# Cross-attention, second pass: blocks 2 to 32 score all 8 key tiles in one go, then weigh their own 8, with nothing carried into the next block

## What is computed

```python
q = ln @ Wq
kv = concatenate([xn, ln]) @ Wkv
k, v = split(kv)                       # 8 heads of 64 each
sim = einsum('bhid,bhjd->bhij', q / scale, k)
sim = sim - max(sim, axis=-1)
attn = softmax(sim, axis=-1)
out = einsum('bhij,bhjd->bhid', attn, v)
out = rearranged(out) @ Wout
```

## Time and profile before

| | |
|---|---|
| median of 3 runs | 2656.38 us (2655.33 to 2661.38) |
| the profiled execution: its own time | 2653.46 us |
| its span, first to last instruction | 2651.8 us |
| mean granted TensorE clock | 0.969 of full |
| TensorE busy | 2490.5 us (94%) |
| VectorE busy | 1809.0 us (68%) |
| ScalarE busy | 1122.2 us (42%) |
| GpSimd busy | 592.2 us (22%) |

### The profile page before, as it was taken

How to read it: one execution, slowest core, us unless ns; L and a number is a source line. 1 busy time by engine, 2 the same in 40 slices (tenths; PEclk the granted TensorE clock), 3 DMA queues, 4 the chain that set the end, 5 groups by cost and what they waited for, 6 DMA issues and landing times.

```text
span 2651.8 us, 33253 instructions
## 1 busy us (share of the span) xinstructions
PE 2490.5 (94%) x11614; PEld 1681.0 (63%) x11618; DVE 1809.0 (68%) x1885; ACT 1122.2 (42%) x1366; POOL 592.2 (22%) x404
## 2 busy tenths in 40 slices
PE   6999989988776999999999999999898899999998
PEld 5778877654334777776655555555586777777775
DVE  5878855499988677778976666666445766666665
ACT  2334422466344222222255555555233455455543
POOL 4555544488842211111100000000000000000000
PEclk9999998999877999999999999999898899999999
DMA  7667755722021343343233232232112255666663
GB/s 276 231 237 259 264 153 171 258 72 72 2 101 42 127 169 148 127 182 136 96 124 108 96 96 73 96 108 84 64 64 115 104 219 214 237 229 230 216 218 137
DMA packets 124235, 394.70 MB, mean 149 GB/s; under 512 B 23728, under 2 KB 39292, under 8 KB 97136
## 3 DMA queue, kind: packets, MB, share of 16 engines
q1 hardware_dynamic: 95584, 326.82, 34.8%
q10 hardware_dynamic: 28560, 66.66, 7.2%
HBM read 304.14 MB, written 89.30 MB: 148 GB/s over the span
## 4 chain that ended last, share of the span: by engine, by line
PE 79%; DVE 8%; DMA 5%; POOL 3%; issue 3%; ACT 2%; ACTq 0%; SPq 0%; DVEq 0%; POOLq 0%
PE ps L2109 18%; PE ps L2110 17%; PE ps L2111 17%; PE ps L2496 10%; PE ps L2506 9%; PE ps L2403 3%; DMA w_halves<-unit_lo 3%; DVE ps L1642 2%; POOL work L951 1%; PE ps L2757 1%; DMA wT_lo<-w_halves 1%; DMA sh_raw<-in_s_parts 1%; DMA x_res<-in_x 1%; POOL work L932 1%; DVE ln_st L1512 1%
## 5 line engine op out<-in xcount | busy, mean ns | idle before, releaser
L1862 DVE TENSOR_TENSOR sums<-sums,pT 128x1024 f32<-128x1024 f32 x272 | 319.2, 1222 | 194.0 <-ACT pT L1341 192.9
L1800 DVE SCALAR_TENSOR_TENSOR peak<-ps,rs_all,peak 128x1024 f32<-128x1024 f32 x272 | 335.7, 1279 | 93.9 <-PE ps L2403 93.6
L1341 ACT ACTIVATE pT<-ps,rs_all 128x1024 f32<-128x1024 f32 x272 | 284.8, 1111 | 230.8 <-PE ps L2496 184.9
L2506 PE MATMUL ps<-pT,values 128*64 128x512 f32 x1088 | 256.4, 602 | 0.0
L2226 PE MATMUL ps<-work,ident 128*128 128x512 f32 x256 | 130.3, 641 | 33.6 <-POOL work L932 18.6
L1001 POOL TENSOR_TENSOR cT_lo<-cT_raw,cT_hi 128x512 fp32r<-128x512 f32 x60 | 77.6, 1293 | 352.1 <-ACT cT_hi L1290 352.1
L2506 PEld LDWEIGHTS ps<-pT,values 128*64 128x64 f32 x1088 | 68.8, 136 | 132.9 <-issue 112.0
L1996 DVE TENSOR_TENSOR rgu_lo<-rgu_raw,rgu_hi 128x2048 fp32r<-128x2048 f32 x64 | 143.9, 2289 | 5.1 <-ACT rgu_hi L1424 5.0
L894 POOL TENSOR_TENSOR ctx_lo<-ctx_raw,ctx_hi 128x512 fp32r<-128x512 f32 x64 | 105.2, 1643 | 131.7 <-DVE ctx_hi L1547 131.7
L1642 DVE TENSOR_TENSOR_SCAN ps<-ps,work 128x1024 f32<-128x1024 f32 x50 | 114.3, 2285 | 13.2 <-ACT ps L1213 11.2
L1028 POOL TENSOR_SCALAR ln_ve<-ln_mv 128x1 f32<-128x1 f32 x4 | 1.5, 379 | 537.0 <-DVE ln_mv L1513 537.0
(11 more groups left out here) (470 smaller groups left out, 6429.9 us busy)
## 6 DMA issues: line engine op xcount, KB each, us to landing
rgu_raw<-in_r_gate_up SPq DMA_DIRECT2D x64, 1024.0 KB, 4.8
rd_raw<-in_r_down SPq DMA_DIRECT2D x32, 1024.0 KB, 4.8
sh_raw<-in_s_parts SPq DMA_DIRECT2D x32, 768.0 KB, 4.3
key_rows<-key_hi SPq DMA_DIRECT2D x17, 1024.0 KB, 3.9
key_rows<-key_lo SPq DMA_DIRECT2D x17, 1024.0 KB, 6.0
value_rows<-values SPq DMA_DIRECT2D x17, 1024.0 KB, 8.9
ctxT_raw<-in_ctx_T SPq DMA_DIRECT2D x16, 1024.0 KB, 6.8
ctx_raw<-in_ctx SPq DMA_DIRECT2D x16, 1024.0 KB, 8.5
```

The lines of the kernel that those rows point to most:

```text
L1341: nc.scalar.activation(pT[:, i], ps[:, b:b + 2], ACT.Exp, scale=rs_all[:, bass.ds(c * KT + attend_tile(j, i)[1], 1)]).then_inc(s4_exp.sem, 1)
L1800: nc.vector.scalar_tensor_tensor(peak[:, p], ps[:, b:b + 2], rs_all[:, bass.ds(c * KT + kt, 1)], peak[:, p], ALU.mult, ALU.max).then_inc(s ...
L1862: nc.vector.tensor_tensor(sums[:, p], sums[:, p], pT[:, i], ALU.add).then_inc(s4_sum.sem, 1)
L2506: done = nc.tensor.matmul(ps[e * DK:(e + 1) * DK, 6 + p], values[:, s, kt, h * DK:(h + 1) * DK], pT[:, i, e], start=start and kt == 0, sto ...
```

## The change

In blocks 2 to 32 all 8 tiles form one group: TensorE scores tiles 0 to 7, then weighs tiles 0 to 7 of the same block, and carries nothing over. Block 2 still begins its weighing with tiles 6 and 7 of block 1. Block 33 keeps its three groups, with nothing to weigh after the first. The weighing waits at first for the exponential of tile 2, and before each of the tiles 3 to 7 for that tile's own. In block 17 the wait for the two copies stands ahead of the weighing, after all 8 tiles are scored. Blocks 2 and 3 are now written out ahead of TensorE's first loop, which runs once less.

```diff
 def attend_groups(j):
 
-    return ((0, 1), (2, 3), (4, 5), (6, 7)) if isinstance(j, int) and j < 2 else ((0, 1, 2), (3, 4, 5), (6, 7))
+    if isinstance(j, int) and j < 2:
+        return ((0, 1), (2, 3), (4, 5), (6, 7))
+    if isinstance(j, int) and j == BLOCKS - 1:
+        return ((0, 1, 2), (3, 4, 5), (6, 7))
+    return (tuple(range(BLOCK)),)
...
             def weigh_values(j, s, half, tiles, start=False, stop=False):
 
-                pe.wait_ge(*s4_exp(j * BLOCK + (tiles[-1] + 1)))
+                pe.wait_ge(*s4_exp(j * BLOCK + (min(tiles[-1], tiles[0] + 2) + 1)))
                 for i in tiles:
+                    if i > tiles[0] + 2:
+                        pe.wait_ge(*s4_exp(j * BLOCK + (i + 1)))
                     p, kt = attend_tile(j, i)
...
-                        if start and g == 1 and half:
-                            pe.wait_ge(*o_saved0(1))
-                            pe.wait_ge(*o_saved1(1))
                         weigh_values(j, s, half, groups[g - 1], start, stop)
                     elif isinstance(j, int) and j == 0:
                         shift_transpose(1)
-                    else:
-                        if isinstance(j, int) and j == 1:
+                    elif isinstance(j, int) and 1 <= j <= 2:
+                        if j == 1:
                             shift_transpose(3)
-                        weigh_values(j - 1, 1 - s, 0 if isinstance(j, int) and j == KCHUNKS else half, (6, 7),
-                                     stop=isinstance(j, int) and j == KCHUNKS)
+                        weigh_values(j - 1, 1 - s, half, (6, 7))
+                if len(groups) == 1:
+                    if start:
+                        pe.wait_ge(*o_saved0(1))
+                        pe.wait_ge(*o_saved1(1))
+                    weigh_values(j, s, half, groups[0], start, stop)
...
-            with pe.Fori(0, LEFT) as q:
-                attend_pe(q * 2 + 2, 1, 0, q * 80 + 112)
-                attend_pe(q * 2 + 3, 0, 0, q * 80 + 112)
-            attend_pe(KCHUNKS - 1, 1, 0, LEFT * 80 + 112)
+            for j in range(2, 4):
+                attend_pe(j, 1 - j % 2, 0, 112)
+            with pe.Fori(0, LEFT - 1) as q:
+                attend_pe(q * 2 + 4, 1, 0, q * 80 + 192)
+                attend_pe(q * 2 + 5, 0, 0, q * 80 + 192)
+            attend_pe(KCHUNKS - 1, 1, 0, LEFT * 80 + 112, stop=True)
```

## The result

| | before | after |
|---|---|---|
| median | 2655.33 us (17 runs) | 2640.37 us (17 runs) |
| ratio of the times | | 0.9949 (95%: 0.9939 to 0.9959) |
| profiled execution, span | 2651.8 us | 2637.0 us |
| second pass, first scoring to reciprocal | 1334.52 to 1866.32, 531.8 us | 1331.40 to 1851.69, 520.3 us |

The change makes the kernel 0.51% faster, 13.5 us by the ratio (10.9 to 16.2). The second pass gave 11.5 us of the gain in the two profiles; the sum had said 11.6. The second pass starts 3.1 us earlier in the profile after, which no edit explains: over the ten profiles of this study its start lies anywhere between 1331.0 and 1336.7.

A forecast was written before the change was run, and what follows sets the result against it. TensorE's own order was taken to bound the kernel: 24.5 us gained on switches and carried weighings, less 12.7 of stall and 0.2 in blocks 17 and 18, is 11.6 off 2656.4, giving 2644.8 us, range 2636 to 2654.

The forecast's parts named there:

- the sum: All terms for the second pass added up: -24.5 + 12.7 + 0.2 = -11.6 us, 0.37 us a block.
- What a switch costs: TensorE between scoring and weighing: 0.37 us a pair of groups beside its tiles; 63 pairs go, 23.3 us.
- The stall: TensorE's scoring overtakes ScalarE's exponentials: tile 7 starts 0.41 us late, 12.7 us lost over 31 blocks.
- The weighing's new waits: Five new waits for exponentials in TensorE's weighing are long satisfied, with a cover of 4 us: cost 0.
- Block 3's load: Block 3's transfers, 6.35 us long, wait for block 1's tiles 6 and 7: cost 0, up to 1 us once.
- Block 17: ScalarE's copy delays exponential 3 and TensorE by 0.60; blocks 17 and 18 give back 0.2 each; together 0.2 lost.
- Block 33: Only six tiles scored in a row; tile 5 is wanted at 4.67 and free at 4.68: cost 0.
- no stall: Rival: ScalarE keeps up or TensorE's depth hides the lateness, all 24.5 us come through, 2631.9 us; chance 0.07.
- The large stall of 0.69: Rival: TensorE's delay a block is 0.69, not 0.41; 2.9 us gained, 2653.5 us; chance 0.17.
- The rule of the Trainium skill: Splitting the array speeds TensorE but not the emptying of PSUM, which may become the limit; scoring then lasts as ScalarE's work.
- this rival: Slower: ScalarE's spacing in the run of eight rises to at worst 1.24 us; 17.6 us lost, 2674; chance 0.10.

The follow-up runs named there:

- Four pairs: The kernel before with four groups of two tiles in every block instead of three, still two tiles carried over: ratio to before 1.0040, 15.67 us a block.
- two gave 15.09: The changed kernel with nothing carried over but blocks 2 to 32 keeping three groups: ratio to before 0.9962, 15.09 us a block.
- the run with half exponentials: The changed kernel with exponentials of half the columns from block 2 on, TensorE's order and waits the same: ratio to before 0.9901.
- a pace of 1.09: One extra one-column ScalarE instruction ahead of each exponential from block 2 on: ratio 0.9994 in the changed kernel, 1.0002 in the kernel before.
- two groups of four: The kernel before with two groups of four tiles in blocks 2 to 32, the second carried into the next block: ratio to before 0.9980.
- Taking the copy out of that place: The changed kernel with block 1's tiles 6 and 7 weighed before block 2's scoring and block 17's copies made before its first exponential: ratio to before 0.9942.

## Why the prediction was right

- *What a switch costs.* 0.37 us a pair of groups, by difference from rows 2. Four pairs gave 15.67, two gave 15.09 with a stall, and the unstalled single pair 14.50. The term of 24.5 us for the switches was a little small: the run with half exponentials gives 24.4 with block 3's wait of 0.7 in it, so 25.1.
- *The stall.* Forecast 0.41 us a block. Measured, it is 0.38 against the sum's own unstalled 7.50 (7.88 or 7.89 less 7.50), and 0.41 against the 7.48 of the run with half exponentials. The handover was 0.06 instead of 0.09, the bare load 0.11 split over two products, and the pace 1.00. What it would have been worth without the stall, and what it does at a pace of 1.09, were both run.
- *The weighing's new waits.* 7.02 us for eight tiles against 7.03: they cost nothing.
- *Block 3's load.* I took 0 with up to 1 us. It slipped by 0.6. What failed was the 6.35 us from issue to landing, read off rows 8. In the kernel before, the traffic of that block does not end at 1379.2: a last part of it runs to 1379.7, 6.8 us after the issue. And a landing comes some 0.5 us behind the end of the traffic, 7.3 us after the issue in the chain after. The expectation for two groups of four left the load out altogether.
- *Block 17.* Forecast a loss of 0.2 in blocks 17 and 18 together. Block 17's scoring took 8.18, 0.3 over an ordinary one, and block 18's 7.67, 0.2 under: a loss of 0.1. Taking the copy out of that place gave 0.5 back.
- *Block 33.* Six tiles scored in a row took 5.67 us, 0.27 less than the two groups before (2.95 and 2.99), without a stall, as the sum had it.
- *The sum.* 11.6 us against 11.5 in the profiles' second pass. That they agree to 0.1 is luck in part: the switches gave about 0.6 more than was put down, and block 3's wait took 0.6 that was not. By the time the gain is 13.5 us, and its interval of 10.9 to 16.2 holds the 11.5. What makes up the two microseconds between, if anything does, stays open. Nothing outside of the second pass was edited, yet that part was 3.3 us shorter in the profile after (2116.7 against 2120.0), within its spread over the ten profiles.

The rivals: no stall was ruled out by the profile after, and the half exponential shows what it would have been. The large stall of 0.69 would have needed 0.13 + 0.35 = 0.48 us from the end of an exponential to the matmuls that waited for it; they start 0.09 after it (1493.09, 1493.18), and the slow second product adds 0.08. ScalarE's pace did not fall in the run of eight: 8.15 us for eight. The rule of the Trainium skill that stood beside this rival, from "TensorEngine Tiling (Array Packing)", section "PSUM Bottleneck", holds: from tile 4 on it is the emptying of PSUM that TensorE waits for.

## What to carry to other kernels

Price a regrouping with two terms: what a switch between two kinds of matmul groups costs, read as the difference between groups of two lengths, and what a longer run asks of the engine that empties PSUM, namely the amount by which its pace is longer than a tile of the run, for each tile past those that its places cover. Here that is about 0.1 us (1.005 against 0.91) from the fifth tile on, with three places. The two balance: a run of four costs 0.37 us for four tiles, and one of eight 0.37 + 0.38 for eight, so past four tiles a longer run gains nothing. And ask of every carried group when its buffer comes free: the load behind it may become the wait.

## What the runs showed that was not expected

- ScalarE's instruction of 0.19 us for one column adds only 0.09 us to the pace when it stands between two exponentials.
- Between the issue of a block's first transfer and the landing of its last lie 7.3 us in the change's block 3, and 7.3 to 8.6 us in the blocks with groups of four whose load is in the chain. The bulk of the traffic is over sooner, but its last part ran to 6.8 us after the issue in the one and to 8.2 in the slowest of the others (1428.2), and the landing came 0.5 us after that in both. A margin read off the end of the bulk is a microsecond or more too wide.
